# Six tiles of dense products in the first stage, low parts ahead of one-hots, and the other tiles' weights fetched at its end

## What is computed

```python
xn = layernorm(x)
W = einsum('rb,bio->rio', comp, basis)          # 8 relation matrices from 4 bases
Hrel = einsum('ni,rio->nro', xn, W)             # node x relation x 256
agg = segment_sum(Hrel[src, edge_type], dst, 2500)
x = x + agg + xn @ loop_weight + bias           # loop_weight: 256 x 256
qkv = xn @ Wqkv.T + bqkv                        # q, k, v of 8 heads, 32 wide
x = x + mix(q, k, v) @ Wproj.T + bproj
...                                             # gated experts, a second layer
```

## Time and profile before

| | us |
|---|---|
| median of 3 runs | 2333.16 |
| the profiled execution | 2337.79 |
| its span, first to last instruction | 2336.1 |
| PE busy | 1982.4 (85%) |
| DVE busy | 1333.4 (57%) |
| ACT busy | 794.8 (34%) |
| POOL busy | 986.4 (42%) |

### The profile page before, as it was taken

How to read it: one execution, slowest core, us unless ns; L and a number is a source line. 1 busy time by engine, 2 the same in 40 slices (tenths; PEclk the granted TensorE clock), 3 DMA queues, 4 the chain that set the end, 5 groups by cost and what they waited for, 6 DMA issues and landing times. The chain is left out here.

```text
span 2336.1 us, 29767 instructions
## 1 busy us (share of the span) xinstructions
PE 1982.4 (85%) x8938; PEld 1271.4 (54%) x8938; DVE 1333.4 (57%) x2919; ACT 794.8 (34%) x2043; POOL 986.4 (42%) x1029
## 2 busy tenths in 40 slices
PE   5666666687888898977997789999998989999999
PEld 2333333444333444466995367666777855565565
DVE  7544444457887888754334678888888842112121
ACT  3111111132433324232443556555553333322322
POOL 6687000076567676402333577777775410000000
PEclk6777777888999999987997989999999989999999
DMA  3233333276566566425222488887785300000000
GB/s 122 84 112 104 121 117 117 118 251 203 149 178 196 169 195 187 137 99 179 72 70 89 163 245 258 235 233 230 221 235 141 110 0 1 10 9 1 9 10 8
DMA packets 138388, 302.93 MB, mean 130 GB/s; under 512 B 27615, under 2 KB 74342, under 8 KB 138102
## 3 DMA queue, kind: packets, MB, share of 16 engines
q0 software_dynamic: 63792, 197.79, 29.7%
q1 hardware_dynamic: 74438, 103.23, 13.3%
HBM read 239.20 MB, written 61.63 MB: 129 GB/s over the span
## 5 line engine op out<-in xcount | busy, mean ns | idle before, releaser
L908 POOL DMA_INDIRECT rows<-h_table,row_rel x352 | 343.3, 975 | 400.3 <-POOLq L111 235.6
L2665 PE MATMUL p_ag<-rows_g,oh_g 128*128 128x260 f32 x1408 | 365.6, 407 | 36.1 <-DVE rows_g L2416 28.4
L2302 POOL DMA_INDIRECT rows_g<-g_table,row_src x352 | 334.9, 951 | 138.7 <-issue 104.5
L2665 PEld LDWEIGHTS p_ag<-rows_g,oh_g 128*128 128x128 f32 x1408 | 252.5, 195 | 117.0 <-issue 64.4
L716 PE MATMUL p_h<-w_rel,xT_f 128*128 128x512 f32 x320 | 192.8, 769 | 129.2 <-DVE h_out L551 126.8
L3032 DVE SCALAR_TENSOR_TENSOR x<-p_yf,cw_f,x 128x256 f32<-128x256 f32 (+1 forms) x160 | 66.4, 477 | 278.6 <-PE p_yf L3192 278.6
L716 PEld LDWEIGHTS p_h<-w_rel,xT_f 128*128 128x128 f32 x320 | 78.1, 252 | 234.2 <-issue 228.8
L2416 DVE TENSOR_TENSOR rows_g<-rows_g,p_e 128x2048 f32<-128x2048 f32 x88 | 200.4, 2277 | 0.2 <-ACT p_e L2518 0.2
L655 ACT CAST h_out<-p_h 128x512 fp32r<-128x512 f32 x80 | 46.9, 587 | 343.1 <-PE p_h L716 314.2
L1069 DVE TENSOR_TENSOR fT<-a_sb,p_sel 128x512 f32<-128x512 f32 x200 | 127.6, 681 | 37.4 <-PE p_sel L1343 37.0
L3192 PE MATMUL p_yf<-f,h_f 128*128 128x256 f32 (+1 forms) x640 | 145.7, 381 | 0.8 <-ACT h_f L3084 0.8
(11 more groups left out here) (513 smaller groups left out, 3565.4 us busy)
## 6 DMA issues: line engine op xcount, KB each, us to landing
h_table<-h_out SPq DMA_DIRECT2D x80, 512.0 KB, 4.1
where_g<-d_table SPq DMA_DIRECT2D x88, 128.0 KB, 4.4
w<-in_L_ffn_W SPq DMA_DIRECT2D x16, 512.0 KB, 9.6
y_table<-yb_g SPq DMA_DIRECT2D x47, 128.0 KB, 1.7
rows<-h_table,row_rel POOLq DMA_INDIRECT x352, 3.7
rows_g<-g_table,row_src POOLq DMA_INDIRECT x352, 4.3
g_table<-row SPq DMA_DIRECT2D x20, 260.0 KB, 2.2
f<-in_L_ffn_W SPq DMA_DIRECT2D x16, 256.0 KB, 5.9
```

The lines of the kernel that those rows point to most:

```text
L908: pool.indirect_dma_start(rows[:, r, j].rearrange("p c d -> p (c d)"), None, st.h_rows, bass.IndirectOffsetOnAxis(ap=st.row_rel[:, at:at + ...
L2302: pool.indirect_dma_start(rows[:, r, j], None, st.g_table, bass.IndirectOffsetOnAxis(ap=st.row_src[:, at:at + 1], axis=0)).then_inc(gather ...
L2665: last = pe.matmul(p_a[:, k % NS, h, 0:HALF], oh[:, r, j], rows[:, r, j, h * HALF:(h + 1) * HALF], start=j % w == 0, stop=j % w == w - 1)
```

## The change

Six tiles' dense products (`EARLY` = 6) go from the second stage into the head of the first. Their weights and biases are loaded there ahead of `src`, `edge_type` and `basis`; PE makes them into the banks `p_h` that the loop uses later (`dense`, two of them behind `count`, the others behind a `turn` each), ACT copies the results out (`taken`), and POOL adds the biases and the loop part. The squares for the norms stay on DVE, in the loop (`squares`, tiles 2 to 7).

To make room in the head, other steps move: `put` runs from tile 5 on instead of tile 10; ACT writes six instead of eight first terms, and behind tile 5 instead of tile 3; DVE makes six relations, three of them between the first maxima and three behind the slots; POOL makes two relations, all four terms of them. The edge records, which DVE made ahead of the second norm, are made behind `scan` and behind `map_ready`.

In the loop, DVE takes the low parts of tile t - 1 ahead of `hots(t)`. At the loop's end SP issues the dense weights, the biases and four turned tiles for the second stage, which keeps them in a buffer `wide` that both stages share. The second stage starts at tile 6 with 14 dense tiles, and its batch lists are written anew: 11 beside dense tiles, 7 in each pair's keys, 12 in each pair's query groups, one left.

```diff
-PUT_FROM = T // 2
+PUT_FROM = 5
-REL_DVE = 5
-REL_EARLY = 2
+REL_DVE = 6
+REL_EARLY = 3
+EARLY = 6
...
         def _(sp):
...
-            sp.dma_start(src_i[:, :], io["src"].rearrange("(p c) -> p c", p=EP)).then_inc(edges_in, 16)
-            sp.dma_start(et_i[:, :], io["edge_type_8"].rearrange("(p c) -> p c", p=EP)).then_inc(edges_in, 16)
...
+            sp.dma_start(w_lv[:, :, 0:D], io["L0_gnn_loop_weight"].rearrange("(k p) o -> p k o", p=P)).then_inc(w_in, 16)
...
+            sp.dma_start(src_i[:, :], io["src"].rearrange("(p c) -> p c", p=EP)).then_inc(edges_in, 16)
...
+            sp.dma_start(st.w_lv[:, :, 0:D], io["L0_gnn_loop_weight"].rearrange("(k p) o -> p k o", p=P)).then_inc(st.w_dense_in, 16)
...
+            for n in range(XR):
+                t = EARLY + n
+                sp.dma_start(st.xT_f[:, t % XR], st.xT_table[t * P:(t + 1) * P, :]).then_inc(xT_in[t % XR], 16)
...
             for q in range(HQ):
                 sp.wait_ge(h_stored[q], 16 * T)
         def _(pool):
...
+            for t in range(EARLY):
+                pool.wait_ge(lv_used, t + 1)
+                x = st.x[:, t * D:(t + 1) * D]
+                pool.tensor_tensor(x, x, loop_p[:, t % 2], ALU.add).then_inc(loop_added, 1)
...
+                if t % 2 and REL_DVE + t // 2 < R:
...
+                    relation(REL_DVE + t // 2)
         def _(dve):
...
-            for r in range(REL_EARLY):
-                relation(r)
...
                 dve.sem_inc(slots_taken, 1)
+                if t % 2 and t // 2 < REL_EARLY:
+                    relation(t // 2)
...
             for t in range(T):
-                hots(t, t % 2)
                 for q in range(4):
                     if t:
                         low_part(t - 1, q)
+                hots(t, t % 2)
+                if 2 <= t < EARLY + 2:
+                    squares(t - 2)
...
         def _(act):
+            def taken(t):
+                act.wait_ge(lv_ready, t + 1)
+                if t >= 2:
+                    act.wait_ge(loop_added, t - 1)
...
         def _(pe):
...
             count()
+            dense(0)
+            dense(1)
             prefix()
             for t in range(GT, T):
                 turn(t)
...
+                if t < GT + EARLY - 2:
+                    dense(t - GT + 2)
...
+            pe.wait_ge(lv_used, EARLY)
+            pe.wait_ge(qk_used, EARLY)
             products(0)
...
 def mix0_and_gather(nc, io, st):
...
-        AT_TILE = (1, 2, 3, 4, 5, 6, 8, 9, 10, 11, 12, 13, 15, 16, 17, 18, 19)
-        AT_KV = [(1, 2, 4, 6, 7, 9)] + [(SEAM, 1, 2, 4, 6, 7, 9)] * (PAIRS - 1)
-        AT_Y = ((0, 3), (1, 4), (0, 2, 4), (1, 4), (1, 3))
+        AT_TILE = (7, 8, 9, 10, 12, 13, 14, 15, 17, 18, 19)
+        AT_KV = [(1, 2, 3, 5, 6, 8, 9)] + [(SEAM, 1, 2, 4, 6, 7, 9)] * (PAIRS - 1)
+        AT_Y = ((0, 3), (0, 2, 4), (0, 2, 4), (1, 4), (1, 3))
...
-            for t in range(T):
+            for t in range(EARLY, T):
                 dense(t)
```

More of the change, by code:

```diff
@@ L207, in slots_and_front @@
         xn = sb("xn", [P, 3, D])
-        xT = sb("xT", [P, XR, D])
+        xT = st.xT
+        loop_p = sb("loop_p", [P, 2, D])
+        b_v = ok_f[:, 0:D]
+        b_qk = sb("b_qk", [P, 2 * D])
         h_out = sb("h_out", [P, HQ, R // HQ, 2, D])
@@ L581, in mixing_constants, with squares @@
                 link(dve.memset(sel[3 * DH:, CH, 0:DH], 1.0))
+            def squares(t):
+                dve.wait_ge(qk_added, t + 1)
+                part = qk_t[:, :, t * DH:(t + 1) * DH]
+                link(dve.tensor_tensor(sq_t, part, part, ALU.mult))
+                link(dve.tensor_reduce(nrm3[:, :, t:t + 1], sq_t, AX, ALU.add))
             for t in range(T):
-                hots(t, t % 2)
                 for q in range(4):
@@ L727, in records, with dense @@
                 last.then_inc(hot_used, 1)
+            def dense(t):
+                if t == 0:
+                    pe.wait_ge(w_in, 48)
+                pe.wait_ge(xT_ready, t + 1)
+                if t >= 2:
+                    pe.wait_ge(lv_used, t - 1)
+                for k in range(K):
+                    last = pe.matmul(p_lv[:, t % 2], xT[:, t % XR, k * P:(k + 1) * P], w_lv[:, k], start=k == 0, stop=k == K - 1)
+                last.then_inc(lv_ready, 1)
+                if t >= 2:
+                    pe.wait_ge(qk_used, t - 1)
+                for k in range(K):
+                    last = pe.matmul(p_qk[:, t % 2], xT[:, t % XR, k * P:(k + 1) * P], w_qk[:, k], start=k == 0, stop=k == K - 1)
+                last.then_inc(qk_ready, 1)
             for t in range(GT):
@@ L734, in _ @@
                 turn(t)
-                if t >= PUT_FROM:
-                    if t == PUT_FROM:
-                        pe.wait_ge(start_ready, 1)
-                        pe.wait_ge(spread_copied, 1)
-                    for n in range(2):
-                        put(2 * (t - PUT_FROM) + n)
+                if t == PUT_FROM:
+                    pe.wait_ge(start_ready, 1)
+                    pe.wait_ge(spread_copied, 1)
+                at = 2 * (t - PUT_FROM)
+                if 0 <= at < T:
+                    put(at)
+                    put(at + 1)
+                if t < GT + EARLY - 2:
+                    dense(t - GT + 2)
             columns()
@@ L807, in mix0_and_gather @@
         dv = sem("dv2")
-        w_in = sem("w_in2")
-        xT_in = [sem(f"xT_in2{r}") for r in range(XR)]
         lv_ready = sem("lv_ready")
@@ L1103, in _ @@
                 one_hot(s)
-            dve.wait_ge(w_in, 80)
-            for t in range(T):
+            dve.wait_ge(st.w_dense_in, 80)
+            for t in range(EARLY, T):
                 dense(t)
-                loops = t + 1
+                loops = t + 1 - EARLY
+                if t == T - 1:
+                    lengths()
                 if t in AT_TILE:
```

160 lines of the change are left out of this document (103 added, 57 removed).

## The result

The changed kernel takes 2151.47 us in the median of four runs (2149.04 to 2161.64) beside 2336.69 us for the kernel before: a ratio of 0.922, 95% interval 0.918 to 0.925. Measured once more with five runs beside the experiments it took 2141.69 us beside 2337.10, a ratio of 0.917 (0.915 to 0.919). The profiled execution took 2150.23 us, its span is 2148.2 us.

A forecast was written before the change was run, and what follows sets the result against it. It took the loop to be bound by a chain of waits, not an engine. Terms -162 - 3 + 4 + 0 - 31 = -192 from 2337.8 gave 2146, and 2142 us for the median; range 2118 to 2192.

The forecast's parts named there:

- The loop: First stage's loop: PE no longer waits, clock at upper level, rounds 10.5 us instead of 19.68; 18 rounds save 162 us.
- The stores: Loop: bank stores must land before ACT's next copy; some rounds late by 1 or 2 us, +4, between 0 and +20.
- the covers: Loop: checks that other work fits the 10.5 us round: DVE 8.0 to 9.9 us, store landings, DMA share about 0.6.
- ACT waiting for stores in most rounds: Loop: one of the signs listed as showing the forecast wrong.
- DVE's 9.9 of 10.5 us: Loop, rounds 2 to 7: DVE's work with squares; where it overflows, DVE sets the round by some tenths.
- The head: First stage before tile 1: slots about 6 us later, 5.5 to 6 given back; total 0, between -6 and +10.
- The second stage: Weights present early -12, six dense tiles fewer -21, sums moved +2, gathers follow: -31 us, between -18 and -42.
- Low clock: Loop: PE still pauses every round, products keep 9.5 us, round 13.1, 47 us more: 2189 us; chance 0.12.
- Scatters set the loop's end: First stage: POOL issues nothing during one-hots, three scatters a round, stage ends some 50 us later: 2192 us; chance 0.05.
- Loop unchanged: Loop: low parts wait for something else, round stays 19.68 us, only second stage gains: 2307 us; chance 0.04.
- Slower by the store ring: Loop: store, copy, low part decide the round; loses if landing passes 19.7 us; 2376 us at 22 us landing; chance 0.03.

The follow-up runs named there:

- the kernel with late weights: Changed kernel with the fetch of dense weights, biases and four turned tiles moved back to the second stage's beginning: 2154.82 us, ratio 0.922.
- the paced kernel: Changed kernel with scatters held to 5.5 for each tile, the last near 270 us: 2134.30 us, ratio 0.914; measured again 2136.29 us.
- the kernel with 120 scatters: Changed kernel with paced scatters, six bank buffers and 11 instead of 12 columns by one-hots, so 120 scatters instead of 100: 2140.58 us, ratio 0.917.
- its own experiments: Fetch moved back to the second stage's beginning, in the changed kernel (2154.82 us) and in the changed kernel with paced scatters (2149.91 us).
- six buffers: Changed kernel with six buffers instead of four for the banks that ACT copies: 2135.42 us, ratio 0.915.
- 20 scatters: Changed kernel with 20 of the 100 scatters, records of the other 80 columns left out: 2137.98 us, ratio 0.915.

## Why the prediction came out as it did

**The loop, right.** The round was to be 6.86 + 3.6 = 10.46 us; undisturbed it is 10.45, and 190.3 us for 18 rounds with the cold beginning where the terms gave 189 + 3.1. Undoing the order alone brings back 353.9 us, doing it alone gives 190.5: no other part of the change is needed.

**The stores, mis-sized.** The term was +4 us, between 0 and +20. In the first profile it is 201.3 - 190.3 = 11.0, in the second 4.2, in the kernel with late weights 3.8 (with the first round left out, which took 12.2 us in the first profile and 10.5 and 13.4 in these, 5.9 and 2.6). The step that failed stands under the covers: late stores were to make "some rounds" late "by 1 or 2 us", from two waits of before, and a DMA share of about 0.6 was taken by bytes. ACT waited 57 times, one round lost 4.3 us, and the share is 0.86. The share by bytes held only where scatters are few (0.62 at 223 GB/s). What was left out is that stores no longer have a pause to land in (4.1 us in the median before, 7.3 and 6.2 in the two profiles after), and that the stores' own packets take longer beside scatters.

"ACT waiting for stores in most rounds" was named as a sign of being wrong. It came, and the forecast held: the paced kernel shows that such waits alone cost nothing. DVE's 9.9 of 10.5 us, named first among the dangers, makes no late round where the stores come in time (10.45 us with squares in the paced kernel). But behind a late store it is what hands the lateness on, in five of PE's seven waits; the prediction had the two dangers apart and they act together.

**The head, right by its parts.** The nine relation steps behind the slots start at 73.05 instead of 66.24, 6.8 us later where 6 was said; ACT's first term holds the first relation back by 4.9 us where 3 was said (DVE's timeline; the second row is that of the nine):

```profile
44.21 3.59 DVE L550 SCALAR_TENSOR_TENSOR wide<-h_out,comp,wide 128x512 f32<-128x512 f32 x3 [4.90 <-ACT wide L723]
...
73.05 7.27 DVE L550 SCALAR_TENSOR_TENSOR wide<-h_out,comp,wide 128x512 f32<-128x512 f32 x9
```

One round of one-hots gives 5.7 to 5.9 back, as the two kernels with the order alone show. Together +0.8.

**The second stage, right.** -32.5 for -31. The fetch gives 10.6 to 13.8 by its own experiments, for 12. With the fetch undone the stage still takes 512.2 and 509.2 instead of 530.8, so the six tiles give 18.6 to 21.6, for 19. The first query products, before and after, split it:

```profile
L1353 PE MATMUL p_y<-fT,kvs x400: 592/643/1116, 626.3 to 990.8; 128*64 128x512 f32 x134
```

```profile
L1439 PE MATMUL p_y<-fT,kvs x400: 592/643/1116, 431.9 to 802.5; 128*64 128x512 f32 x134
```

Ahead of them the stage is 39.5 us shorter (160.4 to 120.9), where 12 + 21 + 6 were said; behind them, where most of the sums come back, 6.9 longer (370.5 to 377.4), for 8. POOL's waits for PE fell to 37.4 for 36, so the gathers did follow.

**The remaining distance.** The pieces miss by 4 us in sum. The other half of the 9.5 us is the step from the profiled execution to the median: 4.6 us were taken off since before's median stood that far below its profiled execution; after's median stands 1.2 above its own. The spread of executions (2134 to 2162 us in the two measurements) makes such a step worth little, and the second median met 2142 by the same spread.

**Rivals.** *Low clock:* out, 0.99. *Scatters set the loop's end:* out for this kernel, the last at 242.5 us against 289.7 for tile 19 (the prediction's sum for it, 155 from 72 on, is 227 and not 235); the mechanism is real, as the kernel with 120 scatters shows, but through their number and pace. Of one-hots that stop POOL the trace shows little: scatters 1.70 us apart, six in a round where that rival had three. POOL's longest halt, 6.54 us ahead of the scatter at 142.70, begins while DVE is idle. The rule of the Trainium skill (SBUF — State Buffer, the warning "DVE blocks DMA") speaks of DVE instructions in a two-port mode, and no trace here shows which of the one-hots are in one; so six in a round speak against the rival and do not test the rule. *Loop unchanged:* out. *Slower by the store ring:* the right ring, and far from that size; landing reached 13.4 us at most, and only from 19.7 on was the kernel to lose against before.

## What to carry to other kernels

Where an engine's queue holds work that waits for the next engine ahead of work that this engine waits for, swapping the two can remove the pause and the low clock that comes with it, as it did here, at no cost; try that first, alone, and read what limits next. When a pause goes, look at what used to land in it: a buffer ring that took 5.3 us in the median of a round of 19.7 became the limit in some rounds of 10.45 with scatters. And look at what stands behind the late step in the next engine's queue, since that passes the lateness on. Spreading a background stream over the time that it has, here 5.5 scatters for a tile instead of as fast as POOL could, or two buffers more, took that limit away.

## What the runs showed of the hardware

A busy share of the DMA engines near one was no sign of a limit: 0.97 with six buffers went with the same 221 GB/s and the same rounds as 0.62 with 20 scatters. The share adds up the times of packets, and it can pass one, as here with six buffers (1.02 at 233 GB/s):

```profile
140.00:180.00 40.00, 40.00 (x152) 24.22 (x151) 35.88 (x80) 8.81 (x15) 30.57 (x24) 1.00 1.02 233
```

Small scatters weigh more than their bytes, and most of that weight falls on other transfers. The two DMA queues from 88.45 to 240 us, with 20 scatters and with paced ones (packets, MB, share; q1 has the stores and the turned tiles, q0 the scatters, and with 20 scatters the three reads of the table too):

```profile
q1 hardware_dynamic: 10800, 33.43, 61.0%
q0 software_dynamic: 480, 0.20, 1.0%
```

```profile
q1 hardware_dynamic: 10608, 33.17, 72.5%
q0 software_dynamic: 2528, 0.13, 4.6%
```

The scatters' own packets add 3.6 points; those of q1, with nearly the same bytes, add 11.5. In the changed kernel q1 takes 87.4% for 29.79 MB. The Trainium skill (DMA: Bandwidth & Descriptors, "Why small descriptors are slow (HBM only)") names a fixed cost for each packet and descriptor. For the scatters' own packets the direction agrees (4.6% for 0.13 MB beside 72.5% for 33.17 MB); what makes the packets of the other queue longer no run shows.
